# Attention with a parallel feed-forward branch on one core: the product with v in two halves, two steps behind the exponentials

## The chip, the cores and the metric

The kernel runs on one core of a Trainium2 chip. The metric is the device time of one execution in microseconds (us). Of the kernel before, three executions were timed, and one more was recorded by the profiler.

## The reference

```python
x  = L0_attn_x                      # (4, 2048, 256), f32
xn = layernorm(x)
x  = x + attn(xn, w_qkv, w_out) + ffn(xn, w_gate, w_up, w_down)

# attn: 16 heads of 16 columns, rotary embedding on q and k
scores = einsum('blhd,bmhd->bhlm', q, k) / 4
out    = einsum('bhlm,bmhd->blhd', softmax(scores), v)
# then out @ w_out.T; ffn is silu(x wg') * (x wu') times wd', hidden 768
```

There are 4 sequences of 2048 tokens and 16 heads, so 64 pairs of sequence and head, each with 2048 x 2048 scores. In this text such a pair is called a head.

## The kernel before, in words

**Stage A** (to about 540 us) does the layer norm, q, k, v and the feed-forward branch, block by block of 512 tokens, and leaves q and k in DRAM, v on chip, and x plus the feed-forward result in DRAM.

**Stage B**, which the change touches, is one software pipeline of steps. A head has TILES = 16 steps, and 64 heads give N1 = 1024 steps, with a few more to drain. Each engine runs the same list of steps (`run_steps`, function `step` of each engine) in its own program order, and semaphores hold them together. A step c of the kernel before does the following.

- **M, the maxima** (PE, `max_half`, L656): scores of 128 query rows against 2048 keys in two halves, M0 and M1, each two products of 512 columns (48 contracted rows) into PSUM banks 0 and 1, or 2 and 3. The two products of a half lie on different halves of the array's rows (0 and 64). DVE reduces each half to a row maximum (L1211, 128x1024). M0 of a step waits until the reduction of the previous half 0 is done, and M1 likewise for half 1. This is step c of the head that comes next.
- **The stabiliser**: after 16 steps DVE reduces the maxima once more (neg_max, L1201), POOL splits them in five small operations (L905 to L916), PE transposes the result (L675), ACT copies it (stabT, L809), and SP writes it into extra rows of q_op with two DMAs (L435). This happens at step 17 of a head (STAB_AT), and takes two places in the ring of banks.
- **S, the scores again** (PE, L707): for the tile that lies FIRST2 = 19 steps back, four products S0 to S3 with 51 contracted rows (the maximum is subtracted through the extra rows), 128 keys by 512 queries each. They go to banks 4, 5 and 6 in turn (RING = 3): S0 of a step reuses the bank whose exponential (exp) was S1's of the step before, S1 that of S2, S2 that of S3, and S3 that of S0 of the same step. S0 and S2 lie on rows from 0, S1 and S3 on rows from 64.
- **exp** (ACT, L817): four a step, from a bank into `probs`, which has two buffers of 2048 columns.
- **PV, the product with v** (PE, `weigh_v`, L691): four fp32 products of 512 columns, each on its own strip of 32 array columns, accumulated over the 16 tiles of a head in bank 7. It handles the tile whose exponentials were made one step before, and waits for all four. The profile shows each fp32 product as two records. The first PV of a head waits until ACT has copied the sums of the head before out of bank 7 (the save, `acc_sb`, L803).
- After the save, SP moves the row sums (L443), DVE takes the reciprocal (L1207, INV_AT, six steps after the save), SP stores and spreads it (L445, L448), POOL multiplies (L930) and SP places the output (L453). The queue of SP is in program order: load_stab(h), load_head(h + 2), place_output(h - 1), and at h = 62 the eight y loads (L460).
- Behind step N1 there are no maxima, and each step gets one projection by w_out (L639, four records). The rest of the projections follow the last step.

PE's order in a step is M0, (transpose), S0, S1, M1, S2, PV, S3. On PE nothing overtakes a wait.

Of the kernel before, what the change touches and what calls it, by code (L numbers as in the profile page):

```python
# [46 lines left out]
LAG = 3  # L47
RING = 3
Y_BUFS = 8
UNROLL = SLOTS * TILES  # L50
PRODUCTS = [(0, 0), (0, 1), (1, 0)]
EXACT_PRODUCTS = [(0, 0), (1, 0)]
# [18 lines left out]
def layer_program(nc, x, w_qkv, w_out, w_gate, w_up, w_down, cos_tab, sin_tab, ident_in, out, y_dram, qk_dram, inv_dram):  # L71
# [17 lines left out]
    def sb(stack, name, shape, dt=F32):  # L89
        return stack.enter_context(nc.sbuf_tensor(name, shape, dt))  # L90
# [103 lines left out]


    sB = ExitStack()
    probs = sb(sB, "probs", [P, 2, TILES * P])

    acc_sb = sb(sB, "acc_sb", [P, 2, BANK])
    sums = sb(sB, "sums", [P, TILES])  # L200
# [15 lines left out]
    def bank(n, cols=BANK):  # L216
        return psum[:, n * BANK:n * BANK + cols]
# [77 lines left out]
    N1 = HEADS * TILES  # L295
    FIRST2 = TILES + LAG
    STAB_AT = TILES + 1
    SAVE_AT = FIRST2 + TILES + 1
    INV_AT = SAVE_AT + 6
    STEPS_B = N1 + (INV_AT - TILES) + 1  # L300

# [189 lines left out]
    def _(pe):  # L491
# [168 lines left out]
        def step(c, i):  # L660
            item = items_before(c)

            def take_bank(item):

                if item >= RING:
                    pe.wait_ge(s2_used, item - RING + 1 + HEAD_ITEMS * SLOTS * i)
                return 4 + item % RING

            if c < N1:
                max_half(c, i, 0)  # L670
            h = head_of(c, STAB_AT)
            if h is not None:
                pe.wait_ge(stab_step, STAB_STEPS * (h + 1 + SLOTS * i))
                b = take_bank(item)
                pe.transpose(bank(b).bitcast(F16)[:, 0:P], stab[:, :, :].rearrange("p a t -> p (a t)"),  # L675
                             identh[:, :]).then_inc(s2_full, STAB_ITEMS)
                item += STAB_ITEMS
            g2 = c - FIRST2

            def weigh_v(g3):  # L680

                if 0 <= g3 < N1:
                    h, t = divmod(g3, TILES)
                    if t == 0:
                        pe.wait_ge(v_ready, h + 1 + SLOTS * i)
                        if h >= 1:
                            pe.wait_ge(acc_saved, h + SLOTS * i)

                    pe.wait_ge(s2_used, items_before(c - 1) + extra_items(c - 1) + 4 + HEAD_ITEMS * SLOTS * i)
                    for j in range(4):  # L690
                        mm = pe.matmul(bank(7)[32 * j:32 * j + 32, :], v_op[:, h % 2, t, :], probs[:, g3 % 2, j * BANK:(j + 1) * BANK],  # L691
                                       start=(t == 0), stop=(t == TILES - 1), tile_position=(0, 32 * j))
                    mm.then_inc(pv_done, 1)

            for j in range(4):
                if j == 2 and c < N1:
                    max_half(c, i, 1)
                if j == 3:
                    weigh_v(g2 - 1)
                if 0 <= g2 < N1:  # L700
                    h, t = divmod(g2, TILES)
                    if t == 0 and j == 0:
                        pe.wait_ge(stab_loaded, 32 * (h + 1 + SLOTS * i))
                    b = take_bank(item)
                    r = HALF * (j % 2)
                    e = r + ROWS + STAB_PARTS
                    pe.matmul(bank(b), k_op[r:e, h % SLOTS, t * P:(t + 1) * P], q_op[r:e, h % SLOTS, j * BANK:(j + 1) * BANK],  # L707
                              start=True, stop=True).then_inc(s2_full, 1)
                    item += 1
            if c > N1:  # L710
                project(c - N1 - 1)

# [8 lines left out]
    def _(act):  # L721
# [69 lines left out]
        def step(c, i):  # L791
            item = items_before(c)

            def arrived(item, n=1):
                act.wait_ge(s2_full, item + n + HEAD_ITEMS * SLOTS * i)
                return 4 + item % RING

            h = head_of(c, SAVE_AT)
            if h is not None:
                act.wait_ge(pv_done, TILES * (h + 1 + SLOTS * i))  # L800
                if h >= 2:
                    act.wait_ge(o_placed, 64 * (h - 1 + SLOTS * i))
                nc.scalar.activation(acc_sb[:, h % 2, :], bank(7), ACT.Copy).then_inc(acc_saved, 1)  # L803
            h = head_of(c, STAB_AT)
            if h is not None:
                if h >= 1:
                    act.wait_ge(stab_loaded, 32 * (h + SLOTS * i))
                b = arrived(item, STAB_ITEMS)
                nc.scalar.activation(stabT[:, :], bank(b).bitcast(F16)[0:STAB_PARTS * TILES, 0:P], ACT.Copy).then_inc(s2_used, STAB_ITEMS)  # L809
                item += STAB_ITEMS  # L810
            g2 = c - FIRST2
            if 0 <= g2 < N1:
                if g2 >= 2:
                    act.wait_ge(pv_done, g2 - 1 + UNROLL * i)
                for j in range(4):
                    b = arrived(item)
                    nc.scalar.activation(probs[:, g2 % 2, j * BANK:(j + 1) * BANK], bank(b), ACT.Exp,  # L817
                                         scale=to_score).then_inc(s2_used, 1)
                    item += 1

# [443 lines left out]
```

## Time and profile before

| | |
|---|---|
| Median of three executions | 3136.37 us (3134.51 to 3140.29) |
| Profiled execution, its own time | 3135.18 us |
| Its span | 3133.4 us |
| PE busy | 2966.5 us, 95% |
| DVE busy | 2816.9 us, 90% |
| ACT busy | 2412.5 us, 77% |
| POOL busy | 430.3 us, 14% |
| Granted PE clock | 1.00 in steady stage B, 0.53 from 540 to 587 us |

The span is from the first to the last profiled instruction. PE is the matrix engine and PEld its weight loads, DVE the vector engine, ACT the scalar engine, SP the queue that issues DMAs. An engine counts as busy from the start to the end of each of its instructions; those of PE and DVE overlap their neighbours, so starts, and not durations, tell the rate. Idle time of an engine that isn't the bound costs nothing. The names M0, M1, S0 to S3 and PV are those of the section above.

### The profile page before, as it was taken

The page shows a single profiled execution, that of the slowest core. Times are in us where ns is not written, and L with a number is a line of the kernel's source. Part 1 is how long each engine was busy: PE and PEld are TensorE (multiplying, and loading weights), DVE is VectorE, ACT ScalarE, POOL GpSimd, SP SyncE. Part 2 cuts the span into 40 slices and gives each one's busy share as a digit, 9 for nine tenths or more (in the row PEclk, how much of TensorE's full clock was granted, in tenths as well). Part 3 has the DMA queues.
Part 4 walks back from the last instruction along what each step waited for, and adds up shares of the span by engine and source line. Part 5 has one row for each costly group of instructions (what it writes and reads, how often), then busy time and mean ns, then how long its engine had stood idle before and what let it go on. Part 6 is the DMA issues. An engine that isn't in the chain of part 4 may idle for free.

```text
span 3133.4 us, 51833 instructions
## 1 busy us (share of the span) xinstructions
PE 2966.5 (95%) x19736; PEld 899.2 (29%) x19736; DVE 2816.9 (90%) x3214; ACT 2412.5 (77%) x4609; POOL 430.3 (14%) x672
## 2 busy tenths in 40 slices
PE   5888988799999999999999999999999999999999
PEld 3555555122222222222222222222222222222225
DVE  6777776999999999999999999999999999999962
ACT  4454444488888888888888888888888888888873
POOL 3445454000000000000000000000000000000000
PEclk8999999799999999999999999999999999999999
DMA  2222222011111111111111111111111111111125
GB/s 95 82 88 86 95 87 84 16 30 29 29 30 29 29 30 29 29 30 29 30 29 29 29 29 29 29 29 29 29 29 29 29 29 29 29 29 29 29 62 169
DMA packets 124540, 136.14 MB, mean 43 GB/s; under 512 B 43265, under 2 KB 103297, under 8 KB 124289
## 3 DMA queue, kind: packets, MB, share of 16 engines
q1 hardware_dynamic: 124288, 132.79, 15.3%
q8 instruction: 157, 2.57, 0.3%
q14 instruction: 95, 0.77, 0.1%
HBM read 88.15 MB, written 34.08 MB: 39 GB/s over the span
## 4 chain that ended last, share of the span: by engine, by line
PE 84%; DVE 6%; POOL 3%; ACT 3%; issue 2%; DMA 0%; SPq 0%; POOLq 0%; DVEq 0%
PE psum L691 33%; PE psum L707 30%; PE psum L656 14%; PE psum L566 2%; PE psum L639 2%; POOL qk_rot L862 2%; PE psum L589 2%; DVE row_max L1211 1%; ACT probs L817 1%; POOL parts L868 1%; DVE y_blk L1132 1%; ACT silu L761 1%; ACT staged L768 1%; DVE rot_s L1110 1%; DVE stats L945 1%
## 5 line engine op out<-in xcount | busy, mean ns | idle before, releaser
L1211 DVE TENSOR_REDUCE row_max<-psum 128x1 f32<-128x1024 f32 x2048 | 2409.8, 1219 | 65.4 <-PE psum L656 41.8
L817 ACT ACTIVATE probs<-psum 128x512 f32<-128x512 f32 x4096 | 2129.7, 602 | 343.3 <-PE psum L707 333.1
L707 PE MATMUL psum<-q_op,k_op 51*128 51x512 f16 x4096 | 1236.6, 383 | 43.2 <-ACT probs L817 20.2
L691 PE MATMUL psum<-probs,v_op 128*32 128x512 f32 x8192 | 1093.0, 605 | 9.0
L656 PE MATMUL psum<-k_op,q_op 48*128 48x512 f16 x4096 | 1033.2, 388 | 21.9 <-DVE row_max L1211 20.2
L707 PEld LDWEIGHTS psum<-q_op,k_op 51*128 51x128 f16 x4096 | 311.1, 94 | 1356.2 <-ACT probs L817 1251.2
L930 POOL TENSOR_TENSOR acc_sb<-acc_sb,inv_rows 128x512 f32<-128x512 f32 x64 | 81.7, 1277 | 1807.3 <-DMA inv_rows<-inv_dram 1807.3
L656 PEld LDWEIGHTS psum<-k_op,q_op 48*128 48x128 f16 x4096 | 213.5, 93 | 316.8 <-DVE row_max L1211 313.6
L691 PEld LDWEIGHTS psum<-probs,v_op 128*32 128x32 f32 x8192 | 163.0, 108 | 260.8 <-issue 260.1
L754 ACT ACTIVATE parts<-qk_rot 128x512 f16<-128x512 f32 x64 | 40.3, 630 | 236.3 <-POOL qk_rot L862 236.3
L566 PE MATMUL psum<-xnT,w 128*128 128x512 f16 x768 | 188.1, 393 | 6.9 <-DVE h L1123 6.9
L1123 DVE SCALAR_TENSOR_TENSOR h<-psum,h_fix,silu 128x512 f32<-128x512 f32 x96 | 69.7, 747 | 123.0 <-ACT silu L761 123.0
L558 PE MATMUL psum<-w,xnT 128*128 128x512 f16 (+1 forms) x768 | 130.0, 330 | 6.9 <-POOL lo_max L855 3.9
L862 POOL TENSOR_TENSOR qk_rot<-rot_c,rot_s 128x512 f32<-128x512 f32 x64 | 81.1, 1267 | 171.0 <-DVE rot_s L1110 166.4
L874 POOL TENSOR_TENSOR hT<-h,hT 128x512 f16<-128x512 f32 x80 | 92.7, 1168 | 76.5 <-ACT hT L747 76.5
L566 PEld LDWEIGHTS psum<-xnT,w 128*128 128x128 f16 x768 | 74.7, 101 | 87.1 <-issue 11.5
L1190 DVE TENSOR_TENSOR y_in<-psum,y_in 128x512 f32<-128x512 f32 x32 | 22.1, 692 | 79.0 <-PE psum L639 79.0
L558 PEld LDWEIGHTS psum<-w,xnT 128*128 128x128 f16 x768 | 73.9, 99 | 62.7 <-issue 12.9
L589 PE MATMUL psum<-wdT,hT 128*128 128x256 f16 x768 | 86.4, 272 | 4.3 <-POOL hT L874 4.3
L905 POOL TENSOR_TENSOR neg_unit<-neg_max,unit 128x16 f32<-128x16 f32 x64 | 14.3, 223 | 551.7 <-DVE neg_max L1201 551.7
L581 PE MATMUL psum<-identh,parts 128*128 128x128 f16 x512 | 41.8, 228 | 42.7 <-ACT staged L768 42.7
L589 PEld LDWEIGHTS psum<-wdT,hT 128*128 128x128 f16 x768 | 74.1, 98 | 15.0 <-issue 4.2
(102 smaller groups left out, 1021.4 us busy)
## 6 DMA issues: line engine op xcount, KB each, us to landing
qk_dram<-staged SPq DMA_DIRECT2D x64, 256.0 KB, 3.3
q_op<-qk_dram SPq DMA_DIRECT2D x128, 128.0 KB
k_op<-qk_dram SPq DMA_DIRECT2D x128, 128.0 KB
x_ln<-in_x SPq DMA_DIRECT2D x16, 512.0 KB, 4.1
x_res<-in_x SPq DMA_DIRECT2D x16, 512.0 KB, 5.0
y_dram<-y_blk SPq DMA_DIRECT2D x16, 512.0 KB, 3.2
k_op<-qk_dram SPq DMA_DIRECT2D x128, 64.0 KB
q_op<-qk_dram SPq DMA_DIRECT2D x128, 64.0 KB
```

Source lines behind the costliest of these rows:

```text
L558: mm = pe.matmul(dst, xnT[:, xp, c, t * P:(t + 1) * P], wqkvT[:, wp, c, e0:e1], start=(c == 0 and n == 0), stop=(c == KT - 1 and n == 2))
L566: mm = pe.matmul(bank(dst), w[:, wp, c, j * P:(j + 1) * P], xnT[:, xp, c, :], start=(c == 0 and n == 0), stop=(c == KT - 1 and n == len(ff ...
L589: mm = pe.matmul(bank(DOWN_BANK[t], D), hT[:, hp, j, t * P:(t + 1) * P], wdT[:, wp, j, :], start=(j == 0 and n == 0), stop=(j == HT - 1 an ...
L656: mm = pe.matmul(bank(2 * half + j), q_op[r:r + ROWS, s, t * P:(t + 1) * P], k_op[r:r + ROWS, s, cols:cols + BANK], start=True, stop=True)
L691: mm = pe.matmul(bank(7)[32 * j:32 * j + 32, :], v_op[:, h % 2, t, :], probs[:, g3 % 2, j * BANK:(j + 1) * BANK], start=(t == 0), stop=(t ...
L707: pe.matmul(bank(b), k_op[r:e, h % SLOTS, t * P:(t + 1) * P], q_op[r:e, h % SLOTS, j * BANK:(j + 1) * BANK], start=True, stop=True).then_i ...
L817: nc.scalar.activation(probs[:, g2 % 2, j * BANK:(j + 1) * BANK], bank(b), ACT.Exp, scale=to_score).then_inc(s2_used, 1)
L862: nc.gpsimd.tensor_tensor(qk_rot[:, t % 2, :], rot_c[:, t % 2, :], rot_s[:, t % 2, :], ALU.add).then_inc(qk_ready, 1)
L874: nc.gpsimd.tensor_tensor(hT[:, 1, j, :], h32[:, j % H_BUFS, :], hT[:, 0, j, :], ALU.subtract).then_inc(hlo_ready, 1)
L930: nc.gpsimd.tensor_tensor(acc_sb[:, u, :], acc_sb[:, u, :], inv_rows[:, :], ALU.mult).then_inc(o_ready, 1)
L1123: nc.vector.scalar_tensor_tensor(h32[:, j % H_BUFS, :], bank(PAIR_BANK[BLK + j] + 1), h_fix[:, j:j + 1], silu[:, j % 2, :], ALU.mult, ALU. ...
L1211: nc.vector.tensor_reduce(row_max[:, hl % 2, t, half:half + 1], psum[:, 2 * half * BANK:(2 * half + 2) * BANK], AX.X, ALU.max).then_inc(s1 ...
```

## The change

PV runs two steps behind the exponentials instead of one (PV_LAG), `probs` gets a third buffer, and PV is done in two halves of 256 columns of each strip: `weigh_v(0)` between S1 and M1, and `weigh_v(1)` after S3. For the first tile of a head (t = 0) nothing is done at the first place and all 512 columns at the second. PE's order in a step becomes M0, (transpose), S0, S1, PVa, M1, S2, S3, PVb. PVa waits for the exponentials of two steps back. ACT waits, ahead of its exponentials, for the PV of three steps back instead of two. SAVE_AT and with it INV_AT come one step later, and the pipeline has one step more. Blank lines apart, this is the diff.

```diff
--- before.py
+++ after.py
@@ -47,6 +47,9 @@
 LAG = 3
 RING = 3
 Y_BUFS = 8
+
+PV_LAG = 2
+PROBS = PV_LAG + 1
 UNROLL = SLOTS * TILES
 PRODUCTS = [(0, 0), (0, 1), (1, 0)]
 EXACT_PRODUCTS = [(0, 0), (1, 0)]
@@ -194,7 +197,7 @@
 
 
     sB = ExitStack()
-    probs = sb(sB, "probs", [P, 2, TILES * P])
+    probs = sb(sB, "probs", [P, PROBS, TILES * P])
 
     acc_sb = sb(sB, "acc_sb", [P, 2, BANK])
     sums = sb(sB, "sums", [P, TILES])
@@ -295,7 +298,7 @@
     N1 = HEADS * TILES
     FIRST2 = TILES + LAG
     STAB_AT = TILES + 1
-    SAVE_AT = FIRST2 + TILES + 1
+    SAVE_AT = FIRST2 + TILES + PV_LAG
     INV_AT = SAVE_AT + 6
     STEPS_B = N1 + (INV_AT - TILES) + 1
 
@@ -677,26 +680,33 @@
                 item += STAB_ITEMS
             g2 = c - FIRST2
 
-            def weigh_v(g3):
-
+            def weigh_v(part):
+
+                g3 = g2 - PV_LAG
                 if 0 <= g3 < N1:
                     h, t = divmod(g3, TILES)
+
+                    if t == 0 and part == 0:
+                        return
                     if t == 0:
                         pe.wait_ge(v_ready, h + 1 + SLOTS * i)
                         if h >= 1:
                             pe.wait_ge(acc_saved, h + SLOTS * i)
-
-                    pe.wait_ge(s2_used, items_before(c - 1) + extra_items(c - 1) + 4 + HEAD_ITEMS * SLOTS * i)
+                    if t == 0 or part == 0:
+                        pe.wait_ge(s2_used, items_before(c - PV_LAG + 1) + HEAD_ITEMS * SLOTS * i)
+                    n0, n1 = (0, BANK) if t == 0 else (part * (BANK // 2), (part + 1) * (BANK // 2))
                     for j in range(4):
-                        mm = pe.matmul(bank(7)[32 * j:32 * j + 32, :], v_op[:, h % 2, t, :], probs[:, g3 % 2, j * BANK:(j + 1) * BANK],
-                                       start=(t == 0), stop=(t == TILES - 1), tile_position=(0, 32 * j))
-                    mm.then_inc(pv_done, 1)
+                        mm = pe.matmul(bank(7)[32 * j:32 * j + 32, n0:n1], v_op[:, h % 2, t, :],
+                                       probs[:, g3 % PROBS, j * BANK + n0:j * BANK + n1],
+                                       start=(t == 0), stop=(t == TILES - 1 and part == 1), tile_position=(0, 32 * j))
+                    if part == 1:
+                        mm.then_inc(pv_done, 1)
 
             for j in range(4):
-                if j == 2 and c < N1:
-                    max_half(c, i, 1)
-                if j == 3:
-                    weigh_v(g2 - 1)
+                if j == 2:
+                    weigh_v(0)
+                    if c < N1:
+                        max_half(c, i, 1)
                 if 0 <= g2 < N1:
                     h, t = divmod(g2, TILES)
                     if t == 0 and j == 0:
@@ -707,6 +717,7 @@
                     pe.matmul(bank(b), k_op[r:e, h % SLOTS, t * P:(t + 1) * P], q_op[r:e, h % SLOTS, j * BANK:(j + 1) * BANK],
                               start=True, stop=True).then_inc(s2_full, 1)
                     item += 1
+            weigh_v(1)
             if c > N1:
                 project(c - N1 - 1)
 
@@ -810,11 +821,11 @@
                 item += STAB_ITEMS
             g2 = c - FIRST2
             if 0 <= g2 < N1:
-                if g2 >= 2:
-                    act.wait_ge(pv_done, g2 - 1 + UNROLL * i)
+                if g2 >= PROBS:
+                    act.wait_ge(pv_done, g2 - PROBS + 1 + UNROLL * i)
                 for j in range(4):
                     b = arrived(item)
-                    nc.scalar.activation(probs[:, g2 % 2, j * BANK:(j + 1) * BANK], bank(b), ACT.Exp,
+                    nc.scalar.activation(probs[:, g2 % PROBS, j * BANK:(j + 1) * BANK], bank(b), ACT.Exp,
                                          scale=to_score).then_inc(s2_used, 1)
                     item += 1
```

## Rows read from the trace of the kernel before

**Rows 1.** Groups of instructions: operation, shapes, count, busy us, mean ns, idle before

```profile
L1211 DVE TENSOR_REDUCE row_max<-psum 128x1 f32<-128x1024 f32 x2048 | 2409.8, 1219 | 65.4 <-PE psum L656 41.8
...
L639 PEld LDWEIGHTS psum<-woT,v_space 128*128 128x128 f32 x192 | 36.2, 190 | 6.1 <-DVE y_in L1190 0.8 <-issue 0.5
```

**Rows 2.** 500 us of steady work: stretch, length, busy PE PEld DVE ACT POOL, clock, DMA, GB/s

```profile
1000.00:1500.00 500.00, 489.66 (x3309) 114.57 (x3309) 486.64 (x438) 434.46 (x850) 33.77 (x89) 1.00 0.12 29
```

**Rows 3.** One line's instructions: ns min/median/max, first and last start us

```profile
L1201 DVE TENSOR_REDUCE neg_max<-row_max x64: 185/186/188, 577.1 to 3027.9; 128x16 f32<-128x32 f32 x64
```

**Rows 4.** Timeline, one steady step: start us, duration us, engine, line, tiles, count, idle

```profile
1505.67 0.39 PE L707 MATMUL psum<-q_op,k_op 51*128 51x512 f16 x1
1505.67 0.60 PE L656 MATMUL psum<-k_op,q_op 48*128 48x512 f16 x2
...
1505.90 0.59 PE L707 MATMUL psum<-q_op,k_op 51*128 51x512 f16 x2
1506.09 2.06 ACT L817 ACTIVATE probs<-psum 128x512 f32<-128x512 f32 x4 [0.33 <-PE psum L707]
...
1506.74 0.09 PEld L707 LDWEIGHTS psum<-q_op,k_op 51*128 51x128 f16 x1 [0.31 <-ACT probs L817]
...
1507.06 1.06 PE L691 MATMUL psum<-probs,v_op 128*32 128x512 f32 x8
...
1508.06 0.39 PE L707 MATMUL psum<-q_op,k_op 51*128 51x512 f16 x1
```

**Rows 5.** Timeline of DVE before the exponentials start

```profile
558.91 8.00 DVE L1211 TENSOR_REDUCE row_max<-psum 128x1 f32<-128x1024 f32 x7
```

**Rows 6.** Timeline of DVE over one head

```profile
1511.09 0.19 DVE L1201 TENSOR_REDUCE neg_max<-row_max 128x16 f32<-128x32 f32 x1
1511.19 4.74 DVE L1211 TENSOR_REDUCE row_max<-psum 128x1 f32<-128x1024 f32 x4
1516.31 7.14 DVE L1211 TENSOR_REDUCE row_max<-psum 128x1 f32<-128x1024 f32 x6 [0.37 <-PE psum L656]
1523.69 11.92 DVE L1211 TENSOR_REDUCE row_max<-psum 128x1 f32<-128x1024 f32 x10 [0.25 <-PE psum L656]
1535.53 0.24 DVE L1207 RECIPROCAL inv_sum<-sums 128x16 f32<-128x16 f32 x1
1535.69 14.27 DVE L1211 TENSOR_REDUCE row_max<-psum 128x1 f32<-128x1024 f32 x12
```

**Rows 7.** Timeline of PE cut so that PV's second pass stands alone

```profile
1507.52 0.61 PE L691 MATMUL psum<-probs,v_op 128*32 128x512 f32 x4
```

**Rows 8.** Timeline of PE, the projections that end the kernel

```profile
3088.83 39.98 PE L639 MATMUL psum<-woT,v_space 128*128 128x256 f32 x184
```

**Rows 9.** Timeline, the stabiliser step of a head

```profile
1512.62 0.22 POOL L916 TENSOR_TENSOR stab<-neg_rem,stab 128x16 f16<-128x16 f32 x1
...
1513.38 0.23 PE L675 MATMUL psum<-identh,stab 128*128 128x128 f16 x1
1513.76 0.26 ACT L809 ACTIVATE stabT<-psum 48x128 f16<-48x128 f16 x1
```

**Rows 10.** Timeline of ACT, the saving step of a head

```profile
1521.36 0.59 ACT L803 ACTIVATE acc_sb<-psum 128x512 f32<-128x512 f32 x1
1521.84 3.70 ACT L817 ACTIVATE probs<-psum 128x512 f32<-128x512 f32 x7
```

**Rows 11.** Timeline of the last head, where projections join the steps

```profile
3023.17 7.22 SPq L460 DMA_DIRECT2D y_in<-y_dram  x8
...
3030.88 1.61 SPq L435 DMA_DIRECT2D q_op<-stabT  x2
...
3038.16 0.99 PE L707 MATMUL psum<-q_op,k_op 51*128 51x512 f16 x3 [1.51 <-DMA q_op<-stabT]
...
3047.10 0.60 PE L707 MATMUL psum<-q_op,k_op 51*128 51x512 f16 x3
...
3050.01 0.60 PE L707 MATMUL psum<-q_op,k_op 51*128 51x512 f16 x3
```

## The prediction

> **What bounds the kernel now.** I read the page and the groups of instructions first: DVE's row reductions alone are busy for 2409.8 us, 1.22 each [rows 1], and the table above gives PE 95% of the span and DVE 90%; neither share decides. The window of steady work says more: DVE is busy 486.64 of 500 us, PE 489.66, ACT 434.46 [rows 2]. A busy PE is not yet a PE at its limit, so I went on to the order in time. One head (16 steps) takes 38.90 us on average, from the first and last of the 64 neg_max: (3027.9 - 577.1) / 63 [rows 3].
>
> The timeline of one step shows a chain [rows 4]. S3, the fourth score product of the step before (L707), starts at 1505.67; its exp starts at 1506.09 (0.42 later) and takes 0.60; S2 of this step needs that PSUM bank, since the ring has three, and starts 0.05 after the exp ends, at 1506.74, with 0.31 of idle weight path put down to ACT. The product with v (PV) starts 0.32 later, at 1507.06, and S3 1.00 later again, at 1508.06. 0.42 + 0.60 + 0.05 + 0.32 + 1.00 = 2.39 us: the step's length. The loop runs through PE and ACT, and PV stands in the middle of it. PE alone would need less: two products on different row halves stream together (S3 with the first M0, M0 with S0, both starting 0.22 apart), so it has 0.22 x 4 (S3/M0, M0/S0, S1, the M1 pair) + 0.32 (S2 and the way to PV) + 1.00 = 2.20, and waits 0.19 ahead of S2.
>
> DVE looks full but isn't. Before exponentials start it alone is the limit, and 7 reductions take 8.00 us [rows 5]: with 1.22 for the last, they start (8.00 - 1.22) / 6 = 1.13 apart, or **2.26 a step**. Two short operations per head add 0.10 (neg_max, 1511.09 to 1511.19) and 0.16 (reciprocal, 1535.53 to 1535.69) [rows 6]. DVE's floor is 32 x 1.13 + 0.26 = 36.45 us a head, 2.45 under what is taken.
>
> **The change, part by part.** *Order and halves.* The new step is M0, S0+S1, PVa, M1, S2+S3, PVb. The number of streamed columns stays. S2 and S3 now stand side by side and start together as S3 and M0 do [rows 4]; PVb lies after S3, so S3's exp runs beside it, and the wait at S2 goes: S2 and S3 start at 1.33 of a step (below), S2's exp 0.42 later, S3's 0.49 behind it (the exps of rows 4 start (2.06 - 0.60) / 3 apart), so it ends at 1.33 + 0.42 + 0.49 + 0.60 = 2.84, which is 0.58 of the next step, and the S2 that needs its bank is due at 1.33.
>
> Cost of a half: the passes of PV start at 1507.06 and 1507.52 [rows 4, 7], and fp32 at 256 columns streams in (39.98 - 0.38) / 183 = 0.216 a pass [rows 8], with weight loads of 190 ns [rows 1] hidden by it. A block of 512 is two passes of 0.43 and 0.14 around them, plus 0.10 of the 0.32 ahead of it (the other 0.22 is S2's streaming). A half is then 1.00 - 2 x 0.214 = 0.57. The added cost is 16 matmul records instead of 8, hence one more entry (0.10) and one more 0.14 around the passes: 0.24 a step. What pays: S2+S3 share 0.22 where S3 shared with M0 and S1, S2 stood alone, one slot of 0.22. PE's new step: M0 0.22, S0+S1 0.22 and 0.10 entry (0.32), PVa 0.57, M1 0.22, S2+S3 0.32, PVb 0.57 = **2.22**, against DVE's 2.26. I take no extra for the two new switches beyond these; bounds from below: none (0.57 already halves only the streaming); from above, a half as dear as a whole PV, 1.00 each, giving 3.08. I take the value that the pass of 256 columns is nearest to.
>
> The Trainium skill bears on this in two places. "TensorEngine Tiling (Array Packing)", Key Properties, says that changing the tile shape drains the engine; the 0.10 ahead of PV and the 0.14 around it are what this trace shows of that, and the step now has four changes for two. "TensorE: Matmul & The Clock Gate", Part 3, says weight loads overlap running matmuls only on other row groups; PV uses all rows, and here row and rule differ, since its second pass starts 0.46 after the first with 0.43 of it streaming. By the rule a step would be 2.42, not 2.22.
>
> *Waits.* PVa asks for exponentials two steps old, so never waits. The third buffer keeps exp's wait where it was: exp of a step needs PV of three steps back, done at the end of the step before, ahead of S0's 0.22 + 0.42. S3 needs exp of S0: 0.22 + 0.42 + 0.60 + 0.05 = 1.29 against its slot at 1.33: met, by 0.04. M1 needs DVE's reduction of the same banks one step back, which ends some 0.5 before. So DVE sets the step: 2.26. PE gains 0.04 a step on it until the reductions hold M0 back, at most 2.26 - 0.42 - 1.22 - 0.06 = 0.56 ahead.
>
> *Stabiliser step, once a head.* Before, four reductions take 1516.31 - 1511.19 = 5.12 where 4.52 would do, 0.60 lost [rows 6], because S1 and M1 queue behind the transpose and ACT's copy: transpose 1513.38, copy 1513.76 for 0.26 [rows 9]. The last POOL operation is done 1.75 after neg_max starts (1512.84) [rows 6, 9]. After, with half 0's reduction at 0 and neg_max at -2.36, POOL is done at -0.61, the transpose runs at -0.55, the copy from -0.29 to -0.03, S1 at 0.02, PVa at 0.34, M1 at 0.91. It is due at 1.13 - 0.42 = 0.71: **0.20 lost**, and PE's lead is used up.
>
> *Saving step, once a head.* ACT's copy of the sums delays exp by 0.48 (1521.36 to 1521.84) [rows 10]; before, six reductions take 1523.69 - 1516.31 = 7.38 where three usual steps take 7.17, 0.21 lost [rows 6]. After: exp of S3(c-1) starts at 0.03, the save at 0.51, exp of S0 at 0.99; S3 can't start before 1.65. Here t = 0, and PV is one block of 512 behind S3: 1.65 + 0.32 + 1.00 = 2.97 to the next M0, due at 2.26 + 0.17 of lead (four steps of 0.04): **0.53 lost**. That is the late thing next: the only step with no PVa to fill the time.
>
> A head: 36.45 + 0.20 + 0.53 = 37.18, less than 38.90 by 1.72. Full steps run from c = 19 to 1023, 62.8 heads: **-108 us**.
>
> *Queues.* Saving and reciprocal come one step later (place_output too), and SP takes it before the next head's stabiliser with some 5 us left; copy_v on POOL likewise. Free, by that slack. Not at the end: the eight y loads are issued behind place_output, from 3023.17 for 7.22 us, and the last stabiliser's DMAs right after, at 3030.88; S0 waits for them until 3038.16 [rows 11]. The loads start about 3.0 later against the steps (one step, 2.26, and 6 x 0.13 that shorter steps take from a fixed DMA chain), so the wait grows by 3.0. *Tail:* steps there take 2.91 (3047.10 to 3050.01) [rows 11]; the new order without M is 1.07 (S3's slot, by exp of S0) + 0.32 + 0.57 + 1.06 (projection) = 3.02, +0.11 x 16 = 1.8; a PV of one more step lands in the tail, 1.1. **+6 us**.
>
> Sum: -102 against the profiled execution's 3135.18 (its span is 3133.4, with 1.8 around it), 3033; the median of the runs is 1.2 above that execution, 3136.37: 3034.
>
> **The rivals.** (1) *PE binds, at 2.27 to 2.33 a step.* For: only 0.04 of room, and switches of a kind the trace has only around 512 columns; S3's slot has 0.04 as well. Against: every term is a measured spacing. DVE's 0.26 vanish in it, the lead too. At 2.27 a head is 36.3 and 1.3 for the two special steps, which have no lead to draw on (0.20 + 0.53 and the lead of 0.56), 37.6, or 3060 with the tail; at 2.32 it is 38.4 (3111). (2) *Slower: the weights of the second pass show.* With 0.22 a pass instead of 0.43, a load that doesn't run beside its pass is exposed once more in each half. Priced as the entry, 0.10, for each of the two added passes the step is 2.22 + 0.20 = 2.42, 0.03 over 2.39, and a head 38.7 and 0.7 for the special steps, 39.4: 3136 + 31 + 6 = 3173. It decides from 0.13 a step. Against: rows 8 have longer loads hidden by such passes; for: those are on whole columns, not on four column tiles that load together. It is the rule of "TensorE: Matmul & The Clock Gate" above; rows 7 speak against it. (3) *The special steps cost nothing,* PE's lead covers them: 36.45 a head, -154 + 6: 2988. Against: 0.53 is far over a lead of 0.17. (4) *Nothing moves:* costs and saved wait cancel at a PE step near 2.35: 3136.
>
> **How the numbers follow.** The forecast, DVE's floor with two small stalls, 0.50; its own range is 3012 to 3055. Rival 1 0.27, rival 3 0.05, rival 4 0.05, rival 2 0.13. The range reaches down into rival 3 (2998) and up through most of rival 1 (3105), which leaves out rivals 2 and 4 and a little of 3. About 0.2% (6 us) is what a measurement of this kernel can tell. Faster: 0.50 + 0.27 + 0.05 = 0.82; same 0.05; slower 0.13.
>
> **What would show it.** DVE's busy share in a steady window up from 97.3% to about 99%; reductions 1.13 apart nearly throughout, with two gaps a head, near 0.2 and 0.5; the weight path of M0 or M1 idle behind DVE, not of S2 behind ACT; PVa to M1 0.57, S2+S3 starting together; a head of 37.2. A distance from PVa's start to M1's above 0.65, or DVE waiting for L656 in every step, would make it wrong in favour of rival 1 or 2. A tail no longer than before would remove the 6 us.

## The result, and the profile after

The changed kernel takes **3056.06 us** (median of four executions, 3054.81 to 3058.88), against 3136.52 for the kernel before: a ratio of 0.9747, 95% interval 0.9735 to 0.9759. The forecast was 3034, between 2998 and 3105. The direction and the mechanism hold; 22 us of the gain did not come, and the result lies just outside the 3012 to 3055 that the prediction named for its main account alone. The profiled execution took 3054.89 us, with a span of 3053.1; it is 80.3 us under that of the kernel before. One of the six executions of e12_after_no_wait, below, took 5671.75 us, which nothing in its kernel accounts for, and it is left out of that kernel's median.

On the page, the row reductions and the product with v now read as follows (columns as in [rows 1]).

```profile
L1222 DVE TENSOR_REDUCE row_max<-psum 128x1 f32<-128x1024 f32 x2048 | 2335.8, 1214 | 51.0 <-PE psum L659 51.0
L699 PE MATMUL psum<-probs,v_op 128*32 128x256 f32 (+1 forms) x15872 | 1296.4, 398 | 0.0
```

The records of PV have nearly doubled (15872 for 8192), and PE is busy with them for 1296.4 us where it was 1093.0, yet the kernel is faster. PE's busy share of the span is 95% in both kernels and says nothing of the gain. The steady stretch that answers to [rows 2], and the 64 neg_max that answer to [rows 3]:

```profile
1000.00:1500.00 500.00, 493.09 (x5027) 151.46 (x5025) 489.18 (x454) 462.78 (x882) 35.27 (x91) 1.00 0.12 31
```

```profile
L1212 DVE TENSOR_REDUCE neg_max<-row_max x64: 186/186/189, 577.9 to 2940.2; 128x16 f32<-128x32 f32 x64
```

DVE is busy 97.8% of the stretch, hardly more than the 97.3% before and short of the 99% that the forecast named as a sign; what changed is that 454 of its instructions fit in where 438 did. A reduction is 1.22 long and overlaps the next by 0.08 when they follow at once, so the busy share hides how densely they stand; the distance of starts shows it. A head takes (2940.2 - 577.9) / 63 = 37.50 us, against 38.90. I had forecast 37.18.

One step in the timeline of PE, to be held against [rows 4]: M0, S0+S1, PVa, M1, S2+S3, PVb, M0.

```profile
1509.80 0.39 PE L659 MATMUL psum<-k_op,q_op 48*128 48x512 f16 x2
1510.02 0.38 PE L717 MATMUL psum<-q_op,k_op 51*128 51x512 f16 x2
1510.33 0.64 PE L699 MATMUL psum<-probs,v_op 128*32 128x256 f32 x8
1510.90 0.39 PE L659 MATMUL psum<-k_op,q_op 48*128 48x512 f16 x2
1511.13 0.41 PE L717 MATMUL psum<-q_op,k_op 51*128 51x512 f16 x2
1511.47 0.64 PE L699 MATMUL psum<-probs,v_op 128*32 128x256 f32 x8
1512.04 0.39 PE L659 MATMUL psum<-k_op,q_op 48*128 48x512 f16 x2
```

PVa to M1 is 0.57, as forecast. The first pair of score products lasts 0.38 in the record and the second 0.41: S3 starts 0.02 behind S2. So PE's step is 2.24 here and not 2.22, against DVE's 2.26; where the 0.02 comes from is one of the errors of the prediction, as will be seen. DVE over one head, against [rows 6]:

```profile
1515.11 0.19 DVE L1212 TENSOR_REDUCE neg_max<-row_max 128x16 f32<-128x32 f32 x1
1515.21 3.48 DVE L1222 TENSOR_REDUCE row_max<-psum 128x1 f32<-128x1024 f32 x3
1518.93 10.28 DVE L1222 TENSOR_REDUCE row_max<-psum 128x1 f32<-128x1024 f32 x9 [0.25 <-PE psum L659]
1529.72 11.41 DVE L1222 TENSOR_REDUCE row_max<-psum 128x1 f32<-128x1024 f32 x10 [0.51 <-PE psum L659]
1541.05 0.24 DVE L1218 RECIPROCAL inv_sum<-sums 128x16 f32<-128x16 f32 x1
1541.20 11.34 DVE L1222 TENSOR_REDUCE row_max<-psum 128x1 f32<-128x1024 f32 x10
1552.58 0.19 DVE L1212 TENSOR_REDUCE neg_max<-row_max 128x16 f32<-128x32 f32 x1
1552.68 1.22 DVE L1222 TENSOR_REDUCE row_max<-psum 128x1 f32<-128x1024 f32 x1
```

The nine reductions from 1518.93 take 10.28: (10.28 - 1.22) / 8 = 1.13 apart, DVE's floor. The rows show two gaps in a head, in the stabiliser's step and in the saving step. Against 1.13 a reduction, three take 1518.93 - 1515.21 = 3.72 where 3.39 would do, **0.33 lost** (forecast 0.20), and nine take 1529.72 - 1518.93 = 10.79 where 10.18 would do, **0.61 lost** (forecast 0.53).

### The profile page after: what moved, and what is told of

Same layout as the page of the kernel before. It is cut to its first block, busy times and chain, and to the rows that moved or that the text cites. A ratio compares the mean times of both kernels' runs of the same rounds, so it can differ in the third digit from the quotient of the medians.

```text
span 3053.1 us, 67192 instructions
## 1 busy us (share of the span) xinstructions
PE 2898.7 (95%) x27416; PEld 1057.6 (35%) x27416; DVE 2743.3 (90%) x3214; ACT 2467.2 (81%) x4609; POOL 429.4 (14%) x672
## 4 chain that ended last, share of the span: by engine, by line
PE 78%; ACT 7%; DVE 6%; POOL 3%; issue 3%; DMA 0%; ACTq 0%; SPq 0%; POOLq 0%; DVEq 0%
PE psum L699 35%; PE psum L659 19%; PE psum L717 16%; ACT probs L828 5%; PE psum L569 3%; PE psum L642 2%; PE psum L592 2%; POOL qk_rot L873 2%; DVE row_max L1222 1%; POOL parts L879 1%; ACT silu L772 1%; DVE y_blk L1143 1%; ACT staged L779 1%; PE psum L584 1%; DVE rot_s L1121 1%
## 5 line engine op out<-in xcount | busy, mean ns | idle before, releaser
L1222 DVE TENSOR_REDUCE row_max<-psum 128x1 f32<-128x1024 f32 x2048 | 2335.8, 1214 | 51.0 <-PE psum L659 51.0
L828 ACT ACTIVATE probs<-psum 128x512 f32<-128x512 f32 x4096 | 2178.3, 597 | 193.6 <-PE psum L717 94.2
L699 PE MATMUL psum<-probs,v_op 128*32 128x256 f32 (+1 forms) x15872 | 1296.4, 398 | 0.0
L717 PE MATMUL psum<-q_op,k_op 51*128 51x512 f16 x4096 | 862.9, 381 | 31.5 <-ACT probs L828 23.3
L659 PE MATMUL psum<-k_op,q_op 48*128 48x512 f16 x4096 | 806.9, 391 | 24.9 <-DVE row_max L1222 20.5
L659 PEld LDWEIGHTS psum<-k_op,q_op 48*128 48x128 f16 x4096 | 196.4, 93 | 895.5 <-issue 526.3
L699 PEld LDWEIGHTS psum<-probs,v_op 128*32 128x32 f32 x15872 | 312.5, 108 | 526.7 <-issue 497.8
L717 PEld LDWEIGHTS psum<-q_op,k_op 51*128 51x128 f16 x4096 | 371.8, 94 | 273.8 <-ACT probs L828 73.6
L772 ACT ACTIVATE silu<-psum,gate_fix 128x512 f32<-128x512 f32 x96 | 64.0, 683 | 13.0 <-PE psum L569 12.1
```

Of the source, the lines that this page charges most:

```text
L659: mm = pe.matmul(bank(2 * half + j), q_op[r:r + ROWS, s, t * P:(t + 1) * P], k_op[r:r + ROWS, s, cols:cols + BANK], start=True, stop=True)
L699: mm = pe.matmul(bank(7)[32 * j:32 * j + 32, n0:n1], v_op[:, h % 2, t, :], probs[:, g3 % PROBS, j * BANK + n0:j * BANK + n1], start=(t == ...
L772: nc.scalar.activation(silu[:, j % 2, :], bank(PAIR_BANK[BLK + j]), ACT.Silu, scale=gate_fix[:, j:j + 1]).then_inc(silu_ready, 1)
L828: nc.scalar.activation(probs[:, g2 % PROBS, j * BANK:(j + 1) * BANK], bank(b), ACT.Exp, scale=to_score).then_inc(s2_used, 1)
L1222: nc.vector.tensor_reduce(row_max[:, hl % 2, t, half:half + 1], psum[:, 2 * half * BANK:(2 * half + 2) * BANK], AX.X, ALU.max).then_inc(s1 ...
```

## The experiments

Each label is a kernel; the edits are to the changed kernel unless said otherwise. A head's time is computed as above from the first and last neg_max of the run's trace.

### What the lag, the halves and their places do

**e1_whole_end:** PV whole, behind S3.

```diff
-                    if t == 0 and part == 0:
+                    if part == 0:
                         return
...
-                    if t == 0 or part == 0:
+                    if part == 1:
                         pe.wait_ge(s2_used, items_before(c - PV_LAG + 1) + HEAD_ITEMS * SLOTS * i)
-                    n0, n1 = (0, BANK) if t == 0 else (part * (BANK // 2), (part + 1) * (BANK // 2))
+                    n0, n1 = 0, BANK
```

> Lag of two and three buffers as in the change, but the product with v whole (512 columns a strip), behind S3. My theory: the halves are there to cover the exponential of S0, which S3 needs. Without PVa ahead of it S3 still can't start before 0.22 + 0.42 + 0.60 + 0.05 = 1.29 of a step, then 0.32 and 1.00 follow: 2.61 a step, 41.8 us a head and more, so about 3320 us, slower than before. Rival: the lag alone frees PE, which has only 1.98 us of work in this order; then DVE sets 2.26 a step and it takes some 3030 us.

Measured: 3407.54 us, ratio 1.0869 (1.0847 to 1.0890). Slower by far, as my theory has it, and by more than I said: a head takes 43.05, and in it the usual step is 2.67, not 2.61. From the timeline of one step:

```profile
1501.22 0.38 PE L717 MATMUL psum<-q_op,k_op 51*128 51x512 f16 x2
...
1501.70 2.06 ACT L828 ACTIVATE probs<-psum 128x512 f32<-128x512 f32 x4 [0.61 <-PE psum L717]
...
1502.36 0.39 PE L717 MATMUL psum<-q_op,k_op 51*128 51x512 f16 x1 [0.32 <-ACT probs L828]
1502.67 0.16 PEld L699 LDWEIGHTS psum<-probs,v_op 128*32 128x32 f32 x8 [0.23 <-issue]
1502.67 1.07 PE L699 MATMUL psum<-probs,v_op 128*32 128x512 f32 x8
```

S0 starts at 1501.22 and its exp at 1501.70, 0.48 later, where my sum had 0.42. S3 then waits for that exp with nothing to do for PE, and PV stands behind it. The halves are thus no detail of the change: the first one is what PE does while the exponential of S0 runs.

**e2_lag_alone:** the edit of e1, so PV is whole again, but it is called ahead of S3 (`if j == 3: weigh_v(1)`), as in the kernel before.

> Lag of two and three buffers, but the product with v whole and in its old place between S2 and S3. My theory: the old loop S3, exp, S2, product with v, S3 is untouched by the lag, since it is S2's bank that it runs through: 2.39 a step as before and about 3136 us (3125 to 3145), with the longer wait of the tail. Rival: the lag is what the change gains by, and it takes about 3056 us.

Measured: 3141.01 us, ratio 1.0019 (1.0009 to 1.0028), and a head of (3027.0 - 575.5) / 63 = 38.91 us. In the steady 500 us PE is busy 489.68 and DVE 486.66, as in [rows 2]. The third buffer and the longer lag alone gain nothing; they cost a little, in the tail: from the last neg_max to the end the profiled execution takes 3135.8 - 3027.0 = 108.8, against 3133.4 - 3027.9 = 105.5.

**e3_halves_lag1:** the two halves, one step behind.

```diff
-PV_LAG = 2
+PV_LAG = 1
```

> The two halves at their two places, but one step behind the exponentials, with two buffers. My theory: PVa must now wait for the exponential of the last S3: from S3's start 0.42 + 0.49 + 0.60 + 0.05 = 1.56, then PVa 0.57 and M1 0.22 to the next S3: 2.36 a step, so with special steps 38.4 to 38.9 us a head, 3110 to 3140 us. The tail is as short as before, as the save is not moved. Rival: the lag doesn't matter, 3056 us.

Measured: 3127.70 us, ratio 0.9978 (0.9969 to 0.9988), in the middle of my range. The timeline shows the wait that the lag removes, ahead of PVa:

```profile
1505.82 0.38 PE L717 MATMUL psum<-q_op,k_op 51*128 51x512 f16 x2
1506.26 0.16 PEld L699 LDWEIGHTS psum<-probs,v_op 128*32 128x32 f32 x8 [0.40 <-ACT probs L828]
```

In the changed kernel the loads of PVa, 0.31 behind S0 at 1510.02, read:

```profile
1510.33 0.16 PEld L699 LDWEIGHTS psum<-probs,v_op 128*32 128x32 f32 x8 [0.29 <-issue]
```

PVa starts 0.44 behind S0, against 0.31, and the idle weight path is put down to ACT, not to "issue". A head takes 38.75. So neither part does much alone: the lag without the halves gives +0.2%, the halves without the lag -0.2%, both -2.5%. The two loops through ACT are different ones, and each part opens one.

### Which engine sets the step

**e4_short_max:** each reduction reads 896 columns of its 1024, and the scale of the exponential is halved. The output is not that of the reference.

```diff
-        step_done(nc.vector.tensor_scalar(exp_scale[:, 0:1], pow_m[:, 0:1], SCALE / QK_SCALE ** 2, None, ALU.mult))
+        step_done(nc.vector.tensor_scalar(exp_scale[:, 0:1], pow_m[:, 0:1], 0.5 * SCALE / QK_SCALE ** 2, None, ALU.mult))
...
-                    nc.vector.tensor_reduce(row_max[:, hl % 2, t, half:half + 1], psum[:, 2 * half * BANK:(2 * half + 2) * BANK],
+                    nc.vector.tensor_reduce(row_max[:, hl % 2, t, half:half + 1], psum[:, 2 * half * BANK:(2 * half + 2) * BANK - 128],
```

> The changed kernel with row maxima over 896 of each 1024 columns, and scores halved ahead of the exponential; the output is not the reference's. A reduction is 128 columns shorter, about 0.13 us, so DVE's floor falls from 2.26 to 2.00 us a step. My theory: PE is right behind DVE, at 2.246 a step by S0, exp, S3, PVb, so the head falls by 0.0 to 0.5 us only, 3025 to 3056 us, with DVE now waiting for L659 in each step. Rival: DVE alone is the bound and PE has room: 0.26 us a step less, some 2800 us.

Measured: 3046.91 us, ratio 0.9718 (0.9699 to 0.9738). DVE has 0.26 us a step less to do and the kernel gains 9 us in all on the changed one, 0.01 a step. A head is 37.41. DVE's timeline now has larger gaps in the two special steps:

```profile
1513.42 9.94 DVE L1222 TENSOR_REDUCE row_max<-psum 128x1 f32<-128x896 f32 x9 [0.80 <-PE psum L659]
1524.21 11.19 DVE L1222 TENSOR_REDUCE row_max<-psum 128x1 f32<-128x896 f32 x10 [0.85 <-PE psum L659]
```

One such reduction lasts 1.09, 0.13 less than before, so 1.13 - 0.13 = 1.00 apart would do. The ten reductions from 1524.21 start (11.19 - 1.09) / 9 = 1.12 apart, 2.24 a step, which is PE's step in the timeline above: PE paces them. The changed kernel has two bounds within 0.02 us of each other.

### The term that was too small

**e9_whole_no_wait:** e1 without one wait of ACT.

```diff
-                if g2 >= PROBS:
-                    act.wait_ge(pv_done, g2 - PROBS + 1 + UNROLL * i)
```

> e1_whole_end without ACT's wait for the product with v of three steps back. PE makes S0 behind that product, so the wait for S0's scores covers it. In e1 the exponential of S0 starts 0.48 us after S0, that of S2 0.41 after S2; 0.42 was my figure for both. My theory: the second wait ahead of S0's exponential makes the difference, and S0's loop is the step in this order, so a step falls from 2.67 to 2.61 and the time by 0.06 x 1005 = 60 us, to about 3347. Rival: the 0.06 comes from PE (S0 and S1 end together) and stays: 3407 us.

Measured: 3338.88 us, ratio 1.0642 (1.0623 to 1.0662): 69 us under e1, where 60 were expected. The step is now 2.61:

```profile
1506.73 0.38 PE L717 MATMUL psum<-q_op,k_op 51*128 51x512 f16 x2
...
1507.15 2.06 ACT L826 ACTIVATE probs<-psum 128x512 f32<-128x512 f32 x4 [0.54 <-PE psum L717]
```

S0 to its exp is 0.42. So the extra 0.06 is no matter of how PE ends S0 and S1. It goes with the second wait in front of the exponential, although the product that it waits for had ended some 0.6 us earlier: in the rows of e1 PV ends at 1502.67 + 1.07 = 1503.74, and the next S0's exponential starts at 1501.70 + 2.67 = 1504.37. The kernel before had this row too, and I read past it: in its tail S0 starts at 3050.01 [rows 11] and the exponential as follows.

```profile
3050.50 1.08 ACT L817 ACTIVATE probs<-psum 128x512 f32<-128x512 f32 x2 [0.84 <-PE psum L707]
```

**e12_after_no_wait:** the changed kernel with the same two lines out and nothing else.

> The changed kernel with nothing else but ACT's wait for the product with v taken out, as in e9 (the wait for S0's scores covers it). My theory: the term of my sum that was too small is the way from S0 to its exponential, 0.48 and not 0.42 us. Without the wait PE's pace is the 2.22 that I forecast, its lead at the saving step is near the 0.17 that I forecast (measured now: 0.09), and DVE's idle 0.51 there falls to about 0.42; with a little at the stabiliser a head falls by 0.1 to 0.15: 3048 us (3045 to 3051). Rival: what I missed lies in the two special steps alone, the wait is covered by DVE as the bound: 3056 us.

Measured: 3048.67 us, ratio 0.9723 (0.9711 to 0.9736), 7 us under the changed kernel. The interval just touches that kernel's, so the time alone would not settle it; the timeline does.

```profile
1505.29 0.39 PE L659 MATMUL psum<-k_op,q_op 48*128 48x512 f16 x2
1505.52 0.38 PE L717 MATMUL psum<-q_op,k_op 51*128 51x512 f16 x2
...
1506.62 0.38 PE L717 MATMUL psum<-q_op,k_op 51*128 51x512 f16 x2
...
1507.51 0.39 PE L659 MATMUL psum<-k_op,q_op 48*128 48x512 f16 x2
```

PE's step is 2.22, and both pairs last 0.38. DVE's idle in the saving step is 0.45 instead of 0.51 (0.42 expected):

```profile
1527.60 11.41 DVE L1220 TENSOR_REDUCE row_max<-psum 128x1 f32<-128x1024 f32 x10 [0.45 <-PE psum L659]
```

The idle at the stabiliser stays at 0.25. A head takes 37.42, 0.08 less than in the changed kernel, where 0.1 to 0.15 were expected. So the second wait is worth about a third of the 22 us by which the forecast was off.

### The special steps and the tail

**e6_save_second:** ACT copies the sums out of bank 7 behind the first exponential.

```diff
-            h = head_of(c, SAVE_AT)
-            if h is not None:
...
+            if h_save is not None and not 0 <= c - FIRST2 < N1:
+                save(h_save)
...
+                    if j == 0 and h_save is not None:
+                        save(h_save)
```

> The changed kernel with ACT's save of the sums behind the first exponential of its step instead of ahead of it. My theory: in that step S3 waits for the exponential of S0, which waits for the save. Behind it, S3 starts 0.35 us earlier, and the product with v then waits for the save until 1.78 of the step: the next M0 comes 0.15 to 0.2 us sooner, DVE's gap of 0.51 falls to about 0.35, and a head by 0.15 to 0.2: 3045 us. Rival: the gap comes from the whole block of 512 columns alone, whatever ACT does: no change.

Measured: 3054.83 us, ratio 0.9744 (0.9729 to 0.9759), no difference that can be told, and a head of 37.46. My estimate was wrong. The timeline of the saving step:

```profile
1524.45 0.39 PE L659 MATMUL psum<-k_op,q_op 48*128 48x512 f16 x2
1524.67 0.38 PE L717 MATMUL psum<-q_op,k_op 51*128 51x512 f16 x2
...
1525.65 0.59 ACT L814 ACTIVATE acc_sb<-psum 128x512 f32<-128x512 f32 x1
...
1525.80 0.09 PEld L717 LDWEIGHTS psum<-q_op,k_op 51*128 51x128 f16 x1 [0.60 <-ACT probs L832]
...
1526.34 1.07 PE L699 MATMUL psum<-probs,v_op 128*32 128x512 f32 x8
1527.34 0.39 PE L659 MATMUL psum<-k_op,q_op 48*128 48x512 f16 x2
```

S3 does come earlier, at 1.35 behind the step's M0 instead of 1.63, but PV must wait for the save, which starts at 1.20 and ends at 1.79, and PV starts at 1.89, where it started at 1.94. The next M0 comes at 2.89 instead of 2.94, no more. The block of 512 behind a wait is the trouble, whichever of the two waits it is.

**e7_first_before_s3:** at t = 0, PV between S2 and S3.

```diff
+            first_tile = (g2 - PV_LAG) % TILES == 0
...
+                if j == 3 and first_tile:
+                    weigh_v(1)
...
-            weigh_v(1)
+            if not first_tile:
+                weigh_v(1)
```

> The changed kernel, but in the first tile of a head the whole product with v stands between S2 and S3, as in the kernel before, instead of behind S3. My theory: it then runs while S3 waits for its exponential: save done at 1.10, product from 1.16 to 2.15 of the step, S3 behind it, next M0 at about 2.4 instead of 2.94. DVE's gap of 0.51 falls to 0.1 or less, a head by 0.5: 3025 us. Rival: the late S3 hands the loss on to the next steps through its exponential, and less than half of it is won.

Measured: 3024.32 us, ratio 0.9646 (0.9631 to 0.9660); a head of 37.01, 0.49 less. The gap in the saving step is gone: nineteen reductions in a row follow the stabiliser's.

```profile
1507.98 21.65 DVE L1227 TENSOR_REDUCE row_max<-psum 128x1 f32<-128x1024 f32 x19 [0.25 <-PE psum L659]
```

**e5_y_later:** `load_y` of the first eight blocks at h = 63, behind load_stab and ahead of place_output, instead of at h = 62.

> The changed kernel with the eight y loads issued behind the last stabiliser's DMAs instead of ahead of them. My theory: the last head's wait for q_op<-stabT (6.5 us in the chain of waits) falls to some 2 us, and the stretch from the last row maximum to the end from 114.1 to about 107 us: 3048 us. Rival: the stabiliser waits for something else than the y loads, or the loads are then late for the output: no change.

Measured: 3051.78 us, ratio 0.9732 (0.9717 to 0.9747): 4 us, which the ratio can't tell from nothing. The chain of waits can. In the changed kernel it had these pieces, from the copy of the last stabiliser on:

```profile
2945.15 1.04 SPq L438
2946.24 6.47 DMA q_op<-stabT
2952.76 0.61 PE psum L717 x2
```

In e5 the chain has no DMA piece there, and from the start of the last row maximum to the end it takes 3051.6 - 2943.3 = 108.3 us instead of 3053.1 - 2939.0 = 114.1. That is 5.8 us, near the 7 expected.

**e8_best:** e5 and e7 together.

> Both the y loads behind the last stabiliser and the first tile's product ahead of S3. The two touch different stretches, so I expect the sum of both gains: 3017 us. Rival: they overlap, and it takes no less than the better of the two.

Measured: 3017.59 us, ratio 0.9624 (0.9610 to 0.9637), 38 us under the changed kernel, where the two alone gave 4 and 32. The gains add.

**e10_stab_order:** e8, with PVa ahead of S1 in the stabiliser's step.

```diff
-                if j == 2:
-                    weigh_v(0)
-                    if c < N1:
-                        max_half(c, i, 1)
+                if j == (1 if head_of(c, STAB_AT) is not None else 2):
+                    weigh_v(0)
+                if j == 2 and c < N1:
+                    max_half(c, i, 1)
```

> e8_best, with PVa between S0 and S1 in the stabiliser's step instead of behind S1. My theory: in that step S1 waits for ACT's copy while PE has PVa to do; done first, PVa covers the wait, M1 comes at 0.8 instead of 1.03 after the reduction's start, and DVE's gap of 0.25 there goes. A head falls by 0.2: 3005 us. Rival: PVa ahead makes S1 and the exponentials late instead and the gap moves on: 3017 us or more.

Measured: 3003.31 us, ratio 0.9569 (0.9556 to 0.9582), a head of 36.79. In most heads the idle at the stabiliser is so small that the timeline runs on over it (a row goes on over idle of less than 0.15), in a few a wide one is left:

```profile
1500.89 25.14 DVE L1227 TENSOR_REDUCE row_max<-psum 128x1 f32<-128x1024 f32 x22
...
1541.36 21.64 DVE L1227 TENSOR_REDUCE row_max<-psum 128x1 f32<-128x1024 f32 x19 [0.31 <-PE psum L659]
```

**e11_no_wait:** e10 without ACT's wait.

> e10_stab_order without ACT's wait for the product with v, as in e9. My theory: PE's own pace falls from 2.246 to 2.22 a step but DVE sets 2.26, so only its lead grows: 0 to 5 us less than e10. Rival: none of it is seen, equal to e10.

Measured: **2993.36 us**, ratio 0.9543 (0.9530 to 0.9556), 10 us under e10, twice what I allowed. A head is 36.68, and the steady stretch and the row that answers to the first of e10's read:

```profile
1000.00:1500.00 500.00, 496.05 (x5156) 156.16 (x5154) 499.52 (x467) 480.18 (x902) 37.98 (x98) 1.00 0.12 31
```

```profile
1532.04 25.06 DVE L1225 TENSOR_REDUCE row_max<-psum 128x1 f32<-128x1024 f32 x22
```

DVE is busy 499.52 of 500 us. The two profiled spans are 11.3 us apart. Of these, 2.8 lie ahead of the first neg_max (579.0 in e10, 576.2 in e11), where this edit changes nothing; over the runs that start lies between 574.7 and 579.3. The heads gained 7.2 and the tail 1.3, against 5.1 and 0.9 in e12. In the heads it is the larger lead of PE, 0.04 a step in place of 0.02, that shows at the stabiliser. At DVE's rate 22 reductions would take 21 x 1.13 + 1.22 = 24.95; they take 25.14 in e10 and 25.06 in e11, and the usual head is 36.61 instead of 36.69. The few heads of e10 that take longer, up to 36.98, are at 36.61 too, all but one. That the lead does it is a reading of the timelines; no run varied the lead by itself, and why a few heads of e10 have the wide gap stays open. This version computes all of the reference and is the fastest of the study, 4.6% under the kernel before, near the end of what this order of work on DVE gives, about 36.5 a head (below).

## Why the prediction was right, and where its sizes were off

- **What bounds the kernel before:** right. The loop S3, exp, S2, PV of 2.39 us is what e2 keeps and e3 replaces by another.
- **DVE's floor of 2.26 as the new step:** right. The reductions of the changed kernel start 1.13 apart, in e11 through nearly whole heads.
- **PE's new step of 2.22:** the mechanism was right and one term too small. The costs of a half, of the pairs and of the two more entries were right to 0.01: PVa to M1 is 0.57. Wrong was "S3 needs exp of S0: 0.22 + 0.42 + 0.60 + 0.05 = 1.29 against its slot at 1.33: met, by 0.04". The 0.42 came from S3's exponential; S0's, the first of ACT's step with two waits ahead of it, starts 0.48 behind its product (e1, e9). So S3 comes at 1.35, late by 0.02, and PE's step is 2.24. It doesn't set the time, DVE does, but PE's lead grows by 0.02 a step instead of 0.04.
- **Saving step, 0.53 lost:** measured 0.61. Nearly all terms hold. In the rows below, M0, S3 and the next M0 of that step, S3 was forecast at 1.65 behind M0 and comes at 1.63, the next M0 at 2.97 and comes at 2.94. The lead was 0.09 and not 0.17: the reduction of this M0 starts at 1526.86 (the eighth start in the row of 10.28 above), 0.51 behind it, where 0.42 is the way that it takes at the least. In e12, with the wait out, DVE's idle there falls by 0.06.

```profile
1526.35 0.39 PE L659 MATMUL psum<-k_op,q_op 48*128 48x512 f16 x2
...
1527.98 0.39 PE L717 MATMUL psum<-q_op,k_op 51*128 51x512 f16 x1 [0.37 <-ACT probs L828]
...
1529.29 0.39 PE L659 MATMUL psum<-k_op,q_op 48*128 48x512 f16 x2
```

- **Stabiliser step, 0.20 lost:** measured 0.33. ACT's copy starts later than I had it, and with it S1, PVa and M1 by 0.12 each:

```profile
1516.95 0.22 PE L678 MATMUL psum<-identh,stab 128*128 128x128 f16 x1
...
1517.29 0.27 ACT L820 ACTIVATE stabT<-psum 48x128 f16<-48x128 f16 x1 [0.17 <-PE psum L678]
```

  With the reduction of half 0 at 1517.47 (the third start in the row of 3.48 above), the copy is at -0.18 where I had -0.29: it starts 0.34 behind the transpose's start, and I had allowed 0.26. The transpose itself is at -0.52, forecast -0.55. No row stands behind the 0.26. The kernel before has 0.38, from 1513.38 to 1513.76 [rows 9], but there ACT is at an exponential until 1513.86, so its copy was held up by more than the transpose; the row bounds the distance from above and would have given 0.32 lost. This is the largest single error in a head. Why ACT is later there than behind a score product was not tried; the wait for the earlier stabiliser's DMAs that stands ahead of this one in the code would fit the finding of e9, as it makes two waits here too.
- **Tail, +6:** measured from the last row maximum, 3133.4 - 3026.7 = 106.7 us before and 114.1 after, **+7.4**. The wait for the stabiliser's DMAs grew by (2952.76 - 2939.0) - (3038.16 - 3026.7) = 2.3, forecast 3.0. Steps there are 3.09 long, forecast 3.02, nearly the same 0.06 again; 16 of them, each 0.18 over the 2.91 before, make 2.9 against 1.8. A PV more was put at 1.1, and the remaining 1.1 I have not followed up.

```profile
2963.47 1.13 PE L642 MATMUL psum<-woT,oT_first 128*128 128x256 f32 x4
...
2966.56 1.13 PE L642 MATMUL psum<-woT,oT_first 128*128 128x256 f32 x4
```

- **The two short operations, 0.26 a head:** measured 0.32. I counted neg_max from its own start to the next reduction, 0.10, but it starts only after the reduction before it has ended, so the overlap of two reductions is lost too. In the rows of DVE above, the last of the ten reductions from 1541.20 ends at 1552.54 and started 1.22 earlier, at 1551.32, and the next one starts at 1552.68: 1.36 apart, 0.22 over 1.13. The reciprocal costs 0.10 and not 0.16: ten reductions start in 1541.20 - 1529.72 = 11.48 where 11.31 would do, and the next ten take 11.34 instead of 11.41. DVE's floor is thus nearer to 36.5 than to 36.45.
- **The sum:** 63 heads by 38.90 - 37.50 = 1.40 are -88.5, the tail is +7.4, and neg_max first comes 0.8 us later: -80.3, the difference of the profiled spans. Of the 22 us between forecast and result the heads make 20, the tail 1.4 and the later start 0.8. A head is 0.32 longer than forecast: 0.13 in the stabiliser's step, 0.08 in the saving step, 0.06 in the short operations, and the rest in 0.01 behind each gap and in a few heads that are longer than the usual 37.47 (up to 37.76), for which I have no cause.
- **The rivals:** rival 1 (PE binds) nearly came true, with PE's step at 2.24 under DVE's 2.26. The time alone doesn't refute it, since its 3060 at 2.27 lies nearer to the measured 3056 than the forecast's 3034. The reductions 1.13 apart do, and e7, which gained 32 us with PE's usual step as it was. Rival 2 (the weights of the second pass show) is refuted: the block PVa takes 0.57, with nothing in it for another load. Its second pass, cut out of the step above, starts 0.24 behind the first.

```profile
1510.57 0.40 PE L699 MATMUL psum<-probs,v_op 128*32 128x256 f32 x4
```

  The Trainium skill says in "TensorE: Matmul & The Clock Gate", Part 3, that weight loads overlap running products only on other row groups. These rows don't agree: all eight loads of PVa lie in the 0.16 from 1510.33, and both passes use all 128 rows. The price from which this rival would decide was summed wrongly too: from PE's 2.22 to 2.39 it is 0.17 a step, not 0.13. Rival 3 (the special steps cost nothing) is what e7, e10 and e11 had to build. Rival 4 (nothing moves) is refuted by the time.

## What to carry to other kernels

When a loop runs through two engines, ask of each wait what the first engine could do while it lasts, and cut the longest piece of independent work so that one part lies in each wait: here the same PV cost 0.24 us a step more in two halves and took the step from 2.39 to DVE's 2.26, while the lag alone gave nothing and the halves alone 0.2%. After such a change look at the steps that are exceptions. At t = 0 the old order, PV ahead of S3, was still the better one and gave 32 us; in the stabiliser's step a new one, PVa ahead of S1, gave 14. And take a latency from the same kind of place, with the same number of waits ahead of it, not from the nearest similar instruction: the 0.42 was that of S3's exponential, while S0's 0.48 stood in the tail of the kernel before.

## What the runs showed of the hardware that was not expected

- A second wait ahead of ACT's exponential costs about 0.06 us, though what it waits for ended some 0.6 us before: from S0's start to its exponential 0.48 with it and 0.42 without (e1, e9), and 69 us over the kernel where this is on the loop. No run varied how long before.
- fp32 products in four column strips, 256 columns each, have their second pass 0.24 us behind the first, with its weights loaded meanwhile on the same rows (the eight loads are over 0.16 after the block's start); the block is 0.57 from its first start to the next product.
- Two engines within 0.02 us a step of each other hide much: taking 0.26 us a step from DVE gained 9 us (e4), while removing a wait that no sum had as a bound gained 7 and 10 (e12, and e11 against e10).
